# Softmax statistics of an int8 attention: where row sums and roundings are computed

## The reference

```
def fake_quant(x, bits=8):
    qmax = 2.0 ** (bits - 1) - 1.0
    scale = jnp.maximum(jnp.max(jnp.abs(x)) / qmax, 1e-08)
    return jnp.clip(jnp.round(x / scale), -qmax - 1.0, qmax) * scale   # straight-through form left out
qkv = fake_quant(x) @ fake_quant(w_qkv) + b_qkv          # x: 32 x 128 tokens, 192 wide; 12 heads of 16
attn = jnp.einsum('bhnd,bhmd->bhnm', fake_quant(q), fake_quant(k)) * hd ** -0.5
attn = fake_quant(jax.nn.softmax(attn, axis=-1))
out = jnp.einsum('bhnm,bhmd->bhnd', attn, fake_quant(v))
out = fake_quant(out) @ fake_quant(w_proj) + b_proj
```

## Time and profile before

| | us |
|---|---|
| median of 3 runs | 2184.8 |
| lowest, highest | 2184.58, 2189.62 |
| the profiled execution | 2190.82 |
| its span, first to last instruction | 2188.6 |
| busy in the span: TensorE, VectorE, ScalarE, GpSimd | 1597.6, 1314.9, 976.5, 392.5 |
| pass b, first to last exponential | 169.07 |

### The profile page before, as it was taken

One profiled execution on the slowest core, in us unless ns is written; L12 is line 12 of the kernel. 1 busy time (PEld: TensorE's weight loads), 2 busy tenths in 40 slices (PEclk: granted clock), 3 DMA queues, 4 the chain that ended last, 5 costly groups with the idle time before them and its releaser, 6 DMA issues.

```text
span 2188.6 us, 35434 instructions
## 1 busy us (share of the span) xinstructions
PE 1597.6 (73%) x12048; PEld 1168.1 (53%) x12048; DVE 1314.9 (60%) x4351; ACT 976.5 (45%) x2770; POOL 392.5 (18%) x482
## 2 busy tenths in 40 slices
PE   0065773966777538888888858888888849999996
PEld 0032222855555425555555536666666637777775
DVE  6779885867777658787888824555556531222211
ACT  0165998933333335555555513333333324344442
POOL 6402332000000000000000000222222212333332
PEclk9995555558778759999999977777777759999998
DMA  3000000059930000000000000000000026777775
GB/s 68 15 1 1 1 1 1 3 105 193 188 54 0 0 1 1 0 0 0 0 0 0 1 1 1 23 22 22 22 22 22 22 86 168 176 176 181 176 184 130
DMA packets 136260, 112.98 MB, mean 52 GB/s; under 512 B 29416, under 2 KB 128456, under 8 KB 136136
## 3 DMA queue, kind: packets, MB, share of 16 engines
q1 hardware_dynamic: 119320, 91.70, 17.9%
q0 software_dynamic: 16864, 20.33, 4.9%
HBM read 69.19 MB, written 45.94 MB: 53 GB/s over the span
## 4 chain that ended last, share of the span: by engine, by line
PE 52%; DVE 24%; ACT 13%; issue 6%; POOL 2%; SPq 1%; DVEq 1%; DMA 0%; another core or an unknown queue 0%; ACTq 0%; POOLq 0%
ACT bank L692 8%; PE bank L2230 7%; PE bank L980 7%; PE bank L2215 5%; PE bank L2219 3%; PE bank L1901 3%; PE bank L939 3%; PE bank L973 2%; PE bank L1567 2%; PE bank L1157 2%; PE bank L1914 2%; DVE WK L1753 1%; DVE WK L1483 1%; DVE R L1483 1%; DVE R L1753 1%
## 5 line engine op out<-in xcount | busy, mean ns | idle before, releaser
L1020 POOL TENSOR_TENSOR WK<-WK,mhalf 128x2 f32<-128x2 f32 (+1 forms) x96 | 77.9, 811 | 946.6 <-DVE WK L1407 344.6
L2267 ACT ACTIVATE R<-bank,WK 128x256 f32<-128x256 f32 x234 | 98.2, 471 | 217.9 <-PE bank L2219 217.9
L2122 DVE SCALAR_TENSOR_TENSOR WK<-bank,R,WK 128x192 f32<-128x192 f32 x78 | 29.0, 414 | 268.5 <-PE bank L2230 268.5
L980 PE MATMUL bank<-WK,R 96*128 96x256 f32 x576 | 178.2, 466 | 15.9 <-ACT WK L946 11.0
L692 ACT ACTIVATE bank<-bank,nbias,sc 128x128 f32<-128x128 f32 x384 | 168.9, 1148 | 22.1 <-POOL nbias L513 22.1
L2230 PE MATMUL bank<-R 128*128 128x192 f32 x936 | 169.1, 331 | 0.0
L2151 POOL DMA_INDIRECT moe_sum<-WK x78 | 121.6, 1559 | 263.5 <-DVE WK L2122 184.6
L692 ACT ACTIVATION_READ_ACCUMULATOR bank<-bank,nbias,sc 128x1 f32 x384 | 163.0, 924 | 0.0
L2230 PEld LDWEIGHTS bank<-R 128*128 128x128 f32 x936 | 150.1, 190 | 13.3 <-issue 13.3
L980 PEld LDWEIGHTS bank<-WK,R 96*128 96x128 f32 x576 | 131.7, 238 | 43.9 <-ACT WK L946 16.0
L939 PE MATMUL bank<-ident,WK 128*96 128x128 f32 x320 | 67.6, 349 | 103.6 <-DVE WK L1003 76.2
(11 more groups left out here) (488 smaller groups left out, 4056.8 us busy)
## 6 DMA issues: line engine op xcount, KB each, us to landing
moe_rows_in<-zeros SPq DMA_DIRECT2D x1, 25026.0 KB, 139.1
R<-in_L_ffn_w SPq DMA_DIRECT2D x39, 576.0 KB
R<-in_L_ffn_w SPq DMA_DIRECT2D x39, 384.0 KB
R<-moe_rows_in SPq DMA_DIRECT2D x39, 194.0 KB, 4.7
R<-in_L_ffn_w SPq DMA_DIRECT2D x78, 96.0 KB
WK<-in_L_ffn_b SPq DMA_DIRECT2D x39, 96.0 KB
moe_sum<-resid POOLq DMA_DIRECT2D x16, 192.0 KB
moe_sum<-WK POOLq DMA_INDIRECT x78, 5.9
```

The source lines that it names most:

```text
L980: mm = nc.tensor.matmul(out, w[0:C, c, m], a.xT[0:C, c, :], start=(c == 0), stop=(c == 1))
L1020: nc.gpsimd.tensor_tensor(a.rs[:, 0:n], a.ve[:, 0:n], mhalf[:, 0:n], ALU.pow).then_inc(f.root, 1)
L2267: ins = nc.scalar.activation(x_hid[q], bank[(0, 2, 0)[p] + n][:, 0:NR], ACT.Gelu, bias=xb_1[h][:, q:q + 1])
```

## The change

Four edits, all in pass b:

- For every fourth unit (u % 4 == 3, a "kept" unit) the three exponentials have no accumulator output. They are written to `ex`, an SBUF buffer of four units that pass c also uses, and VectorE adds them up row by row (`summed`, a tensor_reduce of 128x384) into `sum_all`. A new semaphore `b_sum` counts these sums; ScalarE waits for it before it writes a buffer again.
- `summed` stands in VectorE's list after the maximum and the part of the next kept unit; the sum of unit 127 stands after the loop, ahead of the reciprocal.
- The rounding of queries and keys goes from VectorE to GpSimd (`rounded`), which does it after the `nbias` of every odd unit.
- GpSimd's addition of the bias row goes from units 7 and 15 to units 2 and 10. At the end of a group VectorE writes one element of `amx` and waits for it before it clears its semaphore.

```
-                v.wait_ge(b_taken, r + 1)
-                nc.vector.tensor_scalar(tokens(qk_all, n)[:, k - 2, :], tq[:, k - 2, :], MAGIC, MAGIC, ALU.add,
-                                        ALU.subtract).then_inc(b_qk, 1)
+
+            def summed(U):
+                v.wait_ge(b_exp, U + 1)
+                nc.vector.tensor_reduce(units(sum_all, U // 16, U % 16), ex[:, U // 4 % 4, :].rearrange("p (k n) -> p k n", k=3),
+                                        X, ALU.add).then_inc(b_sum, 1)
...
                     if u % 2 and AHEAD + 8 * g + u // 2 < 8 * NG:
                         part(AHEAD + 8 * g + u // 2)
+                    if u % 4 == 3 and g + u > 3:
+                        summed(16 * g + u - 4)
+                ch.step(nc.vector.memset(amx[:, 3:4], 0.0))
                 ch.clear()
...
+            summed(16 * NG - 1)
+            v.wait_ge(b_sum, 4 * NG)
...
+            def rounded(r):
+                n, k = r // 8, r % 8
+                if n < NG and k >= 2:
+                    pool.wait_ge(b_taken, r + 1)
+                    nc.gpsimd.tensor_scalar(tokens(qk_all, n)[:, k - 2, :], tq[:, k - 2, :], MAGIC, MAGIC, ALU.add,
+                                            ALU.subtract).then_inc(b_qk, 1)
...
+            for r in range(AHEAD):
+                rounded(r)
...
-                    if u in (7, 15):
+                    if u in (2, 10):
                         with_bias(g, u // 8)
+                    if u % 2:
+                        rounded(AHEAD + 8 * g + u // 2)
...
+                    kept = u % 4 == 3
+                    if kept and 4 * g + u // 4 >= 4:
+                        act.wait_ge(b_sum, 4 * g + u // 4 - 3)
                     for k in range(3):
                         s = bank[u % 4][:, k * P:(k + 1) * P]
-                        ins = nc.scalar.activation(s, s, ACT.Exp, bias=nbias[:, u, k:k + 1], scale=col(SS),
-                                                   accum_out=units(sum_all, g, u)[:, k:k + 1])
+                        if kept:
+                            ins = nc.scalar.activation(ex[:, u // 4, k * P:(k + 1) * P], s, ACT.Exp, bias=nbias[:, u, k:k + 1],
+                                                       scale=col(SS))
+                        else:
+                            ins = nc.scalar.activation(s, s, ACT.Exp, bias=nbias[:, u, k:k + 1], scale=col(SS),
+                                                       accum_out=units(sum_all, g, u)[:, k:k + 1])
```

More of the change, by code:

```diff
@@ L282, in tower @@
             "a_xq", "a_xTp", "a_xT", "a_qkp", "a_qk", "a_top", "a_vp", "a_v")]
-        b_sc, b_p, b_taken, b_qk, b_vq, b_sp, b_neg, b_bias, b_exp, b_resid = [sem(n) for n in (
-            "b_sc", "b_p", "b_taken", "b_qk", "b_vq", "b_sp", "b_neg", "b_bias", "b_exp", "b_resid")]
+        b_sc, b_p, b_taken, b_qk, b_vq, b_sp, b_neg, b_bias, b_exp, b_resid, b_sum = [sem(n) for n in (
+            "b_sc", "b_p", "b_taken", "b_qk", "b_vq", "b_sp", "b_neg", "b_bias", "b_exp", "b_resid", "b_sum")]
         c_c, c_ln, c_pt, c_ptTp, c_ptT, c_sp, c_e, c_p, c_op, c_o = [sem(n) for n in (
```

## The result

The changed kernel took 2199.45 us (median of 7 runs, 2194.03 to 2204.52), the kernel before 2185.78 beside it on the same chip (7 runs, 2181.81 to 2192.69). The ratio over all these runs is 1.0054, with a 95% interval of 1.0033 to 1.0074: slower. The forecast was 2175.2, and faster. The profiled execution of the changed kernel took 2199.45, with a span of 2197.8; the one of before was 2190.82. So the medians lie 13.7 apart and the two profiled executions, both at a mean granted clock of 0.811, 8.6; the second is what the changed stage lost.

A forecast was written before the change was run, and what follows sets the result against it. ScalarE's exponentials were taken to set the pace in pass b; -8.7 (kept exponentials) - 2.0 (start) + 0.5 (early waits) + 0.6 (last sum) = -9.6 us, giving 2175.2, with 8 in 10 from 2171 to 2182.

The forecast's parts named there:

- the rounding on GpSimd: Pass b: a rounding of 128x512 moved to GpSimd would take 1.0 us, between 0.49 and 1.23.
- rival (c): GpSimd becomes the bound in units 0 to 11, from 1.57 us a rounding; at 2.0 sum about +9, 2194; chance 0.07.
- kept exponentials: ScalarE, every fourth unit: 96 exponentials without accumulator at 0.35 instead of 0.440 us, saving 8.7, bounds 9.6 and 4.8.
- the start: Ahead of the first unit: first exponential at 196.05 instead of 198.05, as GpSimd rounds while VectorE takes; gain 2.0 us.
- rival (a): Exponentials without accumulator are hardly cheaper, 0.39 us: saving 4.8 instead of 8.7, sum -5.7, 2179; chance 0.10.
- rival (d): Accumulator read is overlapped, so kept exponentials save nothing and stay at 0.44; only the start remains, about -1, 2184; chance 0.05.
- The sums on VectorE: 32 reductions of 128x384 added on VectorE, hidden except unit 127's ahead of the reciprocal: +0.6 us.
- not the bound: VectorE in the pass b stretch: about 130 us busy of some 160 after losing 42 roundings and gaining 32 sums.
- The hidden biases: Biases queued behind GpSimd's roundings come 0.1 us later within a group, against at least 0.76 of ScalarE room: no cost.
- rival (b): GpSimd rounds at about 1.5 us, by its own pace or sharing access with VectorE; sum about -4.3, 2180.5; chance 0.11.
- Line 397 at 0.62 at the borders: Sign at group borders: this VectorE line falls from 1.21 to 0.62 us once the bias-row addition moves away.
- The program's time follows the stage: Everything after pass b is unchanged and only starts earlier, so the stage's -9.6 us is the program's.

The follow-up runs named there:

- seventh experiment: Changed kernel plus 18 GpSimd instructions in a row behind pass b; 512 columns took 1.993 us for the rounding, 1.585 with one operation, 1.04 for a tensor sum.
- first experiment: Changed kernel with all roundings back on VectorE, kept exponentials and sums left in: 2184.08 us against 2191.31 for the kernel before, ratio 0.9969.
- the eighth: Changed kernel with all roundings on VectorE and GpSimd's 3.58 us memset moved into the last group: 2181.34 us against 2188.98 before, ratio 0.9959.
- third experiment: Changed kernel with GpSimd's memset moved from the start of pass b into the last group: 2195.46 us, ratio 1.0017 to the kernel before.
- fifth experiment: Changed kernel with GpSimd rounding only 256 of 512 columns: one rounding 1.085 us, clearing to reciprocal 175.0 us, -7.1 against before.
- fourth experiment: Changed kernel with only 14 of 48 roundings on GpSimd, none ahead of the first unit: 2186.76 us, ratio 0.9978 to the kernel before.
- second experiment: Changed kernel without kept units or VectorE sums, roundings still on GpSimd: 2188.02 us against 2191.31 for the kernel before, ratio 0.9984.
- 6: Changed kernel with GpSimd rounding only 384 of 512 columns: one rounding 1.511 us, clearing to reciprocal 181.5 us, -0.6 against before.
- 9: Kernel before with a pause of 13 ScalarE copies ahead of the first exponential: 2179.99 us against 2169.54, ratio 1.0056.
- 10: Kernel before with a pause of 16 ScalarE copies ahead of the first exponential: 2182.63 us against 2169.54, ratio 1.0073.
- 12: Changed kernel run again without edit on the third chip: 2178.55 us against 2169.54 for the kernel before, ratio 1.0053.

## Why the prediction was wrong

**The step that failed** is the rounding on GpSimd, "I take 1.0", with 1.23 as "the upper bound". It measured 1.937. The bound came from line 507, and took for granted that a column with one input costs no more than one with two. The seventh experiment shows it the other way: per 512 columns the sum of two tensors costs 1.04, one operation with a scalar 1.59, two 2.0. The row was from another kind of instruction, and nothing in the trace tied the two kinds together; a bound needs that. The one GpSimd row of the right kind was line 513, 3 columns in 0.30, which says nothing of the price of a column. The honest upper end was open, and rival (c) was given 0.07 with the remark "It needs a rounding twice as long as the add of two inputs"; that is what came (1.937 against 0.992). The rule of GPSIMD Engine Reference in the Trainium skill (Key points) that was set beside it, about twice VectorE's time, was too kind as well: it is 1.937 against 0.494.

**What happened was rival (c)**, GpSimd as the bound. The parts of the measured +8.7 are +5.7 before the first exponential, -8.7 from the kept exponentials, +11.0 in the groups and +0.6 for the last sum. The forecast had -2.0, -8.7, +0.5 and +0.6. So two terms were off, the start by 7.7 and the groups by 10.5. That rival (c) names nearly the same sum, +9, is in part luck: it was worked out for 2.0 us. With the measured 1.937 its own steps give -2.0 + 5.6 for the start and 7 x (6 x 0.37 - 0.8) = 9.9 for the groups, with the other terms about +6. The rest is the late start of the first rounding, 2.0, which it did not have, and about 1 more in the groups. Its point of no return, 1.57 us, fits the sizes tried: one wait of 0.34 at 1.085, 3.2 us at 1.511 (0.06 below it, where the bunches of addition and rounding already show), 9.4 at 1.937.

**The kept exponentials, -8.7: right.** 1.03 for three (0.34 each, where line 2258 had given 0.35), and in the first experiment 160.4 us in place of 169.07 for all exponentials, which makes 0.35 each. The 0.39 of rival (a) and rival (d), in which they pay nothing, fell with that. The estimate of 0.387 that the prediction drew from ScalarE: Activation LUTs in the Trainium skill (What ACT_TABLE_LOAD costs) was too high by 0.04; the measurement decides.

**The sums on VectorE, hidden but for the last, +0.6: right.** 0.54 each, and the last stands in the chain with 0.56 in the changed kernel, in the first experiment and in the eighth.

**VectorE, "not the bound": right, and worth more than the prediction made of it.** It was computed as 130 busy of 160 with the roundings gone. With them kept it is 138 of 157 (first experiment), and still hidden. The prediction never asked what the forecast would be without the move; the answer is the first experiment, -8.1 counted from the clearing of the sums, which is the forecast's -8.7 + 0.6.

**The start, -2.0: wrong, by 7.75.** 5.6 come from the longer roundings. 2.0 are a cost that no step had: the rounding is now the first instruction with a scalar behind the reduction over partitions, a configuration comes ahead of it (recorded at 183.2), and 7 us pass before it starts. The kernel before has the same configuration, at 183.4, but asks for its first bias only at 197.64. The first rounding, put at 188.5, came at 190.51. The third experiment shows that it is not the memset that takes this time, and the seventh, where no take comes first, has 7.5 us in the same place.

**The hidden biases: wrong.** "0.1 later, against a room that is nowhere under 0.76" holds for 1.0 us (the fifth experiment, no wait at a border) and not for 1.94: a bias then comes 1.0 later than before. The fourth shows that this needs no full GpSimd; long instructions ahead of a short one are enough.

**Contention, the other half of rival (b): not the cause here, but there.** GpSimd's rounding takes 1.93 whether VectorE is busy (248.17) or idle, as it was from 194.1 to 202.7 while four of the first six ran; VectorE's takes (line 402), which read a bank, last 0.803 beside it and 0.802 before. "Line 397 at 0.62 at the borders" came true: the addition no longer stands beside it. But the changed kernel leaves VectorE hardly an instruction from SBUF to SBUF that could meet a rounding. Where it has one the two do collide: in the second experiment a rounding of values (0.56 alone) lasts 0.92 beside GpSimd's first roundings, and in the fourth VectorE's roundings and the biases behind them are stretched.

**The program's time follows the stage: right**, with the second experiment as the one exception, whose cause stays open: at a higher granted clock its later stages took 13.1 us less.

## What to carry to other kernels

Before an operation is moved to another engine, look for a row of the same kind of instruction on that engine, at a similar width; if there is none, the upper bound is open, and an instruction of another kind gives no end to it. An engine that is idle for two thirds of a stage is still no free place for long work when it also holds a short step that the pacing engine waits for: what counts is what can stand ahead of that step, here 1.9 us against a room of 0.8. And ask of each part of a change whether the others need it: here the part that pays had no need of the part that costs.

## What the runs showed of the hardware

- GpSimd, 128 partitions, f32 input: the operation with scalars costs 1.59 us for 512 columns with one operation, 1.94 to 2.04 with two, 1.09 to 1.16 for 256 columns with two; the sum of two tensors 1.04 for 512. VectorE does the two-operation form in 0.43 alone and 0.494 on average, a quarter. GPSIMD Engine Reference in the Trainium skill (Engine selection) has one-input operations at roughly line rate and two-input ones at half of VectorE's. For two inputs these traces agree, 0.992 against 0.559 for a VectorE operation on two tensors of 128x384 (line 443); for one input they do not.
- From the configuration on GpSimd's queue to the first instruction with a scalar behind it 6.9 to 7.3 us passed in all seven traces in which that instruction could have run sooner (the changed kernel twice, experiments 2, 3, 5, 6 and 7), and 7.5 at a second place in the seventh.
- A memset on GpSimd of 3.58 us held a 3-column instruction on VectorE for 3.43 us; with the memset away it took 0.17. SBUF — State Buffer in the Trainium skill (SBUF: two separate sides) tells of a port pair that one of the two engines holds for a whole instruction while the other is blocked, and the pair of rows looks like that. So do VectorE's roundings in the fourth experiment, 0.87 beside the addition where they take 0.43 alone. One place does not: in the changed kernel lines 397 and 398 of VectorE ran in their usual 0.62 and 0.56 us from 192.91 on, inside a GpSimd rounding that took 2.12 in place of 1.93. The takes, which read PSUM, were never stretched.
- A wait of ScalarE for a bias cost some 0.1 us more than its recorded length: 171.4 us of exponentials against 160.4 with 9.4 us of waits in 15 places, 163.7 with 2.7 in 7 (fourth experiment).
- The mean granted clock of an execution moves the time as much as this change did: the kernel before, on the third chip, took 2162.5 to 2165.7 us in three runs at 0.821 to 0.822 and 2168.0 to 2172.6 in six at 0.812 to 0.814. The kernels of 9, 10 and 12 had no run above 0.813 there, so beside the six their medians stand 9.4, 12.1 and 8.0 us later. With a change of 0.5% the stage's own times in the trace say more than a few runs of the whole.
